# Attention quotients by compacting DMAs and a spreading product in place of transposes, with the jobs spread anew over the steps

## What is computed

```python
xn = layernorm(x)
q = rope(xn @ Wq); k, v = split(ctx @ Wkv); k = rope(k)
w = softmax(q k^T / 4)                    # per head, 256 x 256
attn = (w v) @ Wout + bout
x = x + tanh(g_xattn) * attn
h = layernorm(x)
y = square(relu(h @ up)) @ down + (h @ expert_weight) * (sum of the two largest of h @ gate)
out = x + tanh(g_ffn) * (layernorm(y) * gamma + beta)
```

## Time and profile before

| | |
|---|---|
| median of 3 runs | 1609.11 us (1608.59 to 1610.73) |
| profiled execution | 1609.51 us, its span 1607.7 us |
| mean granted clock of TensorE | 0.991 |
| PE busy | 1552.5 us, 97%, 9818 matmuls |
| DVE busy | 976.1 us, 61% |
| ACT busy | 638.1 us, 40% |
| POOL busy | 296.2 us, 18% |
| DMA | 119.50 MB in 67064 packets on SP's queue |
| first phase | to about 762 us, an iteration in its middle 44.96 us |

### The profile page before, as it was taken

One profiled execution on the slowest core, in us unless ns is written; L12 is line 12 of the kernel. 1 busy time (PEld: TensorE's weight loads), 2 busy tenths in 40 slices (PEclk: granted clock), 3 DMA queues, 4 the chain that ended last, 5 costly groups with the idle time before them and its releaser, 6 DMA issues.

```text
span 1607.7 us, 26049 instructions
## 1 busy us (share of the span) xinstructions
PE 1552.5 (97%) x9818; PEld 1158.5 (72%) x9818; DVE 976.1 (61%) x1448; ACT 638.1 (40%) x962; POOL 296.2 (18%) x370
## 2 busy tenths in 40 slices
PE   8799999999999999988999999999999999999997
PEld 6466666666666666654887887878878878788786
DVE  7887777887887777765663535426444354353524
ACT  4365555555555555556442222222222222222221
POOL 5222222222222222201010102002010020010202
PEclk9799999999999999999999999999999999999999
DMA  6644443444444344333530101101000011010101
GB/s 173 142 114 109 108 102 104 126 104 124 127 124 116 97 107 102 96 89 117 154 105 1 53 27 33 47 2 53 27 27 33 21 47 33 14 46 21 53 0 40
DMA packets 67192, 121.24 MB, mean 75 GB/s; under 512 B 12280, under 2 KB 25720, under 8 KB 67064
## 3 DMA queue, kind: packets, MB, share of 16 engines
q1 hardware_dynamic: 67064, 119.50, 27.8%
HBM read 51.17 MB, written 16.78 MB: 42 GB/s over the span
## 4 chain that ended last, share of the span: by engine, by line
PE 84%; DVE 11%; issue 2%; ACT 1%; POOL 1%; DMA 0%; POOLq 0%; DVEq 0%; ACTq 0%; SPq 0%
PE pP L986 16%; PE pA L1183 11%; PE pO L986 11%; PE pB L1183 11%; PE pT L986 10%; PE pO L1108 6%; PE pA L1080 6%; DVE mneg L1402 5%; PE pM L986 4%; PE pB L1096 2%; PE pT L993 2%; PE pP L993 2%; PE pM L993 2%; PE pM L1150 1%; DVE rot L1330 1%
## 5 line engine op out<-in xcount | busy, mean ns | idle before, releaser
L1402 DVE TENSOR_REDUCE mneg<-pA 128x4 f32<-128x1024 f32 x250 | 305.6, 1223 | 137.1 <-PE pA L1080 135.3
L887 ACT ACTIVATE probs<-pB 128x1024 f32<-128x1024 f32 x249 | 255.2, 1025 | 259.5 <-PE pB L1096 249.4
L1505 DVE TENSOR_TENSOR relu<-relu 128x512 f32<-128x512 f32 x128 | 89.0, 695 | 257.4 <-ACT hid L939 257.4
L704 POOL TENSOR_SCALAR var_eps<-meanvar 128x1 f32<-128x1 f32 x96 | 34.5, 360 | 1048.4 <-DVE meanvar L1287 1048.2
L1183 PE MATMUL pA<-dn,hid 128*128 128x512 f32 x768 | 198.6, 394 | 0.7
L1183 PE MATMUL pB<-dn,hid 128*128 128x512 f32 x768 | 196.0, 390 | 0.0
L986 PE MATMUL pP<-fT,up 128*128 128x512 f32 x768 | 190.3, 396 | 0.0
L986 PE MATMUL pO<-fT,up 128*128 128x512 f32 x768 | 187.6, 393 | 0.0
L1183 PEld LDWEIGHTS pA<-dn,hid 128*128 128x128 f32 x768 | 143.2, 188 | 35.7 <-DVE hid L1507 4.2
L986 PEld LDWEIGHTS pO<-fT,up 128*128 128x128 f32 x768 | 144.3, 188 | 32.6 <-issue 0.7
L1183 PEld LDWEIGHTS pB<-dn,hid 128*128 128x128 f32 x768 | 144.2, 188 | 31.0
(11 more groups left out here) (199 smaller groups left out, 1971.3 us busy)
## 6 DMA issues: line engine op xcount, KB each, us to landing
stk<-kT SPq DMA_DIRECT2D x180, 128.0 KB, 2.9
stq<-qT SPq DMA_DIRECT2D x180, 128.0 KB, 3.0
fres<-x_scratch SPq DMA_DIRECT2D x34, 256.0 KB, 2.8
xin<-x SPq DMA_DIRECT2D x32, 256.0 KB, 3.0
xres<-x SPq DMA_DIRECT2D x32, 256.0 KB, 3.3
x_scratch<-xres SPq DMA_DIRECT2D x32, 256.0 KB, 2.3
out<-y_s SPq DMA_DIRECT2D x32, 256.0 KB, 2.0
fx<-x_scratch SPq DMA_DIRECT2D x29, 256.0 KB, 2.7
```

What stands on the lines that cost most here:

```text
L704: nc.gpsimd.tensor_scalar_add(var_eps[:], meanvar[:, 1:2], EPS).then_inc(ve_made, 1)
L887: nc.scalar.activation(probs[:, s % 4, :, :, :].rearrange("p a b s -> p a (b s)"), psum[:, :, :], ACT.Exp).then_inc(exp_done, 1)
L1402: nc.vector.tensor_reduce(mneg[par][:, :, 2 * u:2 * u + 2].rearrange("p t q -> p q t"), psum[:, :, :].rearrange("p q (t k) -> p q t k", t= ...
L1505: nc.vector.tensor_tensor(r[:], r[:], r[:], ALU.mult).then_inc(sq_made, 1)
```

## The change

The numerators and denominators never leave the layout in which heads lie on partitions. For each half h of a batch (16 heads):

- `gather_den`, one DMA: the 16 denominator rows of `av_s` (4 partitions x 4 column blocks x 256) become `den`, 64 partitions x 64.
- `reciprocals` on DVE: three operations of 64x64 (reciprocal, rounded part, rest), in step 11 for half 0 and in step 3 of the next iteration for half 1.
- `scatter_recips`, two DMAs: rounded part and rest to 32 rows of 256 (`recips`).
- `move_av`, four DMAs: the 16 rows of numerators of each of the four heads in a column to every fourth partition of `numer`, so that 128 partitions are full.
- job b0 or b1 in bank T: two products of 256 columns of a 0/1 matrix (`spread`, 32 rows, made once by POOL) with `recips`. This copies each head's reciprocal onto its 16 partitions; hi and lo are added by the same product.
- DVE multiplies the bank by `numer` (in place), ACT rounds it (`round_av`, steps 4 and 8), POOL takes the rest (`rest_av`). O0 and O1 now take slices of the result, with the rows of Wout reordered on the host.

The jobs a00, a10, a01, a11, aT0, aT1 are gone, and O0, O1, V0, V1 have other steps. Some SBUF tiles have other places (`rot21`, the tiles of m's transposes, which now share their partitions with `recips` and `spread`, and the gate's weights); the two halves of a tile of raw weights lie in `numer`.

```diff
 SCHEDULE = {
-    0: ("X0", "a10"),
+    0: ("X0",),
     1: ("K0",),
-    2: ("Q0<", "a01"),
+    2: ("Q0<", "b0"),
     3: ("m1", "Q0"),
-    4: ("a11",),
+    4: ("V1",),
     5: ("X1", "kT0"),
-    6: ("aT0",),
+    6: ("b1",),
     7: ("K1", "Q1<"),
-    8: ("Q1", "O0<"),
-    9: ("kT1", "O0"),
+    8: ("Q1",),
+    9: ("kT1", "O0<"),
     10: ("qT0",),
-    11: ("aT1", "V1"),
+    11: ("O0",),
     12: ("m0", "qT1"),
-    13: ("O1",),
-    14: ("V0",),
-    15: ("a00",),
+    13: ("V0",),
+    14: ("O1<",),
+    15: ("O1",),
 }
+RECIPROCALS = {11: 0, 3: 1}
+ROUNDED = {4: 0, 8: 1}
...
+            def gather_den(b, h):
+                sp.wait_ge(av_taken, GROUPS * b + GROUPS // 2 * (h + 1))
+                if some(2 * b + h):
+                    sp.wait_ge(rc_in, 2 * INC * (2 * b + h))
+                    alone(sp)
+                sp.dma_start(den[:, :], av_s[HD:P:32, GROUPS // 2 * h:GROUPS // 2 * (h + 1), :]
+                             .rearrange("j g (r s) -> j (g r) s", r=4)).then_inc(den_in, INC)
+
+            def scatter_recips(b, h):
+                n = 2 * b + h
+                sp.wait_ge(rc_made, 3 * (n + 1))
+                if some(n):
+                    freed, of = ("b0", b) if h else ("b1", b - 1)
+                    sp.wait_ge(done[BANK[freed]], number(freed, of))
+                alone(sp)
+                for k, part in enumerate((den_hi, den_lo)):
+                    sp.dma_start(recips[NH // 2 * k:NH // 2 * (k + 1), :].bitcast(F32), part[:, :].bitcast(F32)).then_inc(rc_in, INC)
+
+            def move_av(b, h):
+                sp.wait_ge(av_taken, GROUPS * b + GROUPS // 2 * (h + 1))
+                if some(b):
+                    sp.wait_ge(done[BANK["O1"]], number("O1", b - 1))
+                alone(sp)
+                for j in range(MOVES):
+                    sp.dma_start(numer[j:P:4, 2 * h:2 * h + 2, :].rearrange("p c s -> p (c s)"),
+                                 av_s[32 * j:32 * j + HD, GROUPS // 2 * h:GROUPS // 2 * (h + 1), :]
+                                 .rearrange("d g s -> d (g s)")).then_inc(moved[h], INC)
...
+                if within(bt):
+                    gather_den(bt, 1)
                 if within(b1) and not opened("kT1", b1):
                     load_stack(b1, (par + 1) % 2, 1, "k")
+                if within(bt):
+                    scatter_recips(bt, 1)
+                    move_av(bt, 1)
+                if within(b1) and not opened("kT1", b1):
                     load_stack(b1, (par + 1) % 2, 1, "q")
...
+                gather_den(i, 0)
+                if within(b2):
+                    load_stack(b2, par % 2, 0, "k")
+                scatter_recips(i, 0)
                 if within(bt):
                     store_x1(bt, 0)
-                if within(b2):
-                    load_stack(b2, par % 2, 0, "k")
                 if within(b1):
                     load_max(b1, (par + 1) % 2, 0)
                 if within(b2):
                     load_stack(b2, par % 2, 0, "q")
+                move_av(i, 0)
                 if within(bt):
                     store_x1(bt, 1)
...
+            def rest_av(b, h):
+                pool.wait_ge(at_hi, 2 * b + h + 1)
+                cut = slice(2 * h, 2 * h + 2)
+                nc.gpsimd.tensor_tensor(aT_lo[:, cut, :], numer[:, cut, :], aT_hi[:, cut, :].bitcast(F32),
+                                        ALU.subtract).then_inc(at_lo, 1)
...
+                    for c in range(2):
+                        last = nc.tensor.matmul(psum[:, c * S:(c + 1) * S], spread[:, c, :], recips,
+                                                start=True, stop=True)
...
+                    nc.vector.tensor_tensor(numer[:, cut, :], psum.rearrange("p (c s) -> p c s", c=2), numer[:, cut, :],
+                                            ALU.mult).then_inc(freed, 1)
+
+            def reciprocals(b, h):
+                n = 2 * b + h
+                dve.wait_ge(den_in, INC * (n + 1))
+                alone(dve)
+                d = den[:, :]
+                nc.vector.reciprocal(d, d).then_inc(rc_made, 1)
+                dve.wait_ge(rc_made, 3 * n + 1)
+                nc.vector.tensor_copy(den_hi[:, :], d).then_inc(rc_made, 1)
+                dve.wait_ge(rc_made, 3 * n + 2)
+                nc.vector.tensor_tensor(den_lo[:, :], d, den_hi[:, :].bitcast(F32), ALU.subtract).then_inc(rc_made, 1)
```

More of the change, by code:

```diff
@@ L109 @@
 CUT = [x[:-1] for names in SCHEDULE.values() for x in names if x[-1] == "<"]
-TWO_STEP = ("X0", "X1", "qT0", "qT1", "kT0", "kT1", "aT0", "aT1", "m0", "m1")
+TWO_STEP = ("X0", "X1", "qT0", "qT1", "kT0", "kT1", "m0", "m1")
 ROPES = ("K0", "Q0", "K1", "Q1")
-A_JOBS = ("a00", "a10", "a01", "a11")
+R_AT = HALF_ROWS
+R_ROWS = 2 * NH // 2
+MOVES = 4
 X_AT = (6, 8, 10, 12)
@@ L261, in flamingo_gated @@
         raw1 = [probs[:, k // 2, k % 2, :, :].rearrange("p t s -> p (t s)") for k in range(8)]
-        raw1 += [attn[0][:], attn[1][:], xres[0][:], xres[1][:]]
+        raw1 += [numer[:, 2 * k:2 * k + 2, :].rearrange("p c s -> p (c s)") for k in range(2)]
+        raw1 += [xres[0][:], xres[1][:]]
         rot_k1 = raw1[0]
@@ L365, in flamingo_gated @@
         t_hi = sem("t_hi")
-        rd_made = sem("rd_made")
+        spread_made = sem("spread_made")
+        den_in = sem("den_in")
+        rc_made = sem("rc_made")
+        rc_in = sem("rc_in")
+        moved = [sem(f"moved{h}") for h in range(2)]
+        at_hi = sem("at_hi")
+        at_lo = sem("at_lo")
         res_in = [sem(f"res_in{t}") for t in range(2)]
@@ L736, in iteration @@
                 if prepares:
-                    for name in ROPES[1:]:
-                        rope_sum(b2, name)
+                    rope_sum(b2, "K1")
+                ending = isinstance(i, int) and i == B - 1
+                if ending:
+                    for u in range(2):
+                        inv_std(NT + u + 1)
+                if within(bt):
+                    rest_av(bt, 1)
+                if prepares:
+                    rope_sum(b2, "Q1")
                 if within(i + 3):
@@ L741, in iteration @@
                     split_ctx(i + 3, (par + 1) % 2)
-                if isinstance(i, int) and i == B - 1:
-                    for u in range(UT):
+                if ending:
+                    for u in range(2, UT):
                         inv_std(NT + u + 1)
@@ L1049, in compute @@
                 elif name[0] == "O":
-                    last = product(psum, lambda a, c: aT[a][:, c, :], lambda w, c: wo_s[w][:, c, :], KC, half)
+                    pe.wait_ge(at_lo, 2 * b + (1 if half == 0 else 2))
+                    cut = slice(t * P, (t + 1) * P)
+                    last = product(psum, lambda a, c: aT[a][:, c, cut], lambda w, c: wo_s[w][:, c, :], KC, half)
                 elif name[0] in "qk":
@@ L1202, in fblock @@
                     if first_block and m == 0:
-                        job("a10", B, B)
+                        job("b0", B, B)
                         pe.wait_ge(av_taken, GROUPS * B)
@@ L1206, in fblock @@
                     if first_block and m == 0:
-                        job("a01", B, B)
                         pe.wait_ge(gt_lo, 1)
@@ L1428, in iteration @@
                         ln_apply(i + 3, 0)
+                    if s in RECIPROCALS and within(i - RECIPROCALS[s]):
+                        reciprocals(i - RECIPROCALS[s], RECIPROCALS[s])
                     if planned(norm_at, i, s) is not None:
@@ L1464, in _ @@
             phase1(dve, iteration, ahead=1)
-            job("a00", B - 1)
+            job("O1", B - 1)
             split_gate()
-            job("a10", B)
+            job("b0", B)
             dve.wait_ge(av_done, GROUPS * B)
@@ L1500, in fblock @@
                     if first_block and m == 0:
-                        job("a01", B)
                         for key in ffn_chunks[4:ahead_w]:
```

109 lines of the change are left out of this document (67 added, 42 removed), and 8 rows, old and new, of tables (BANK, LAG).

## The result

The changed kernel takes 1724.91 us (median of 4 executions, 1723.67 to 1727.22) against 1609.55 us before (4 executions): ratio 1.072, 95% interval 1.0704 to 1.0736, so 7% slower. The profiled execution took 1723.87 us, 114.4 more than that of before, with a span of 1722.1.

A forecast was written before the change was run, and what follows sets the result against it. It took TensorE (PE), busy 97% of the span, as the bound. Terms -54 - 12 + 29 + 20 + 36 + 16 + 6 + 15 = +56 on 1609.51 gave 1665 us, range 1630 to 1682.

The forecast's parts named there:

- V0 behind qT1: Step 13, bank P: V0 waits 2.06 us for qT1's evacuation in 14 iterations, +29 us.
- V1 behind m1: Step 4, bank M: V1 waits 1.33 us for m1's evacuation, delayed by DVE's reciprocals, in 15 iterations, +20 us.
- SP's queue: Step 8's logits wait 2.8 us for m1's maxima copies, behind new DMAs, in 13 iterations, +36 us.
- The clock: Behind PE's new long waits the granted clock falls to 1.2 GHz: 9 falls of 1.7 us, +15 us.
- The count of one in three: Two of six earlier PE waits were followed by a clock fall, so 27 new waits over 2 us give 9.
- the clock falls at almost every long wait: Rival: 27 falls of 1.7 us cost 46 us in place of 15, giving 1696 us; chance 0.12.
- The PE work: Transposes that go save 61.3 us, 64 added products of 256 columns cost 7.3 us: -54 us.
- The two ends: Last two iterations, with step 8's copies late by about 5 and 11 us, +16; second phase's first block, +6 us.
- the old waits: Step 0's wait for maxima and step 5's for Q0's rotation go: 0.86 us in 14 iterations, -12 us.
- The rival that SP's chain is in time: m1's maxima copies land before step 8's logits need them, so that wait goes: 1612 us; chance 0.27.

The follow-up runs named there:

- the second run: The changed kernel with only V1's bank changed, from M to T: 1725.22 us, ratio 1.0709 to the kernel before.
- The version of 1599.56 us: Changed kernel with V0, V1 in bank T, m1's copies earlier on SP, residual adds behind Q1's sum, reciprocals in step 2, last iteration's loads and reciprocals reordered: ratio 0.9932.

## Why the prediction was wrong

The direction was right, the time was 60 us short, and the value lay outside the range. The waits were found and sized rightly; two terms of the sum were not: what the low clock costs, and what PE's work gives.

**V0 behind qT1**: 2.06 us x 14 forecast, 28.0 in 14 waits measured. **V1 behind m1**: 1.33 x 15 forecast, 17.7 in 14 measured, with DVE's three operations at 0.94 us where I took 0.85. **SP's queue**: 2.8 us x 13 forecast, 35.8 in 13 measured. From the first scatter (430.74) to the start of the last copy (442.4) SP took 11.7 us where I had 11.2, and that copy was used 2.0 us after its issue where I had 2.5: two errors that cancel, which is luck. The Trainium skill's 2.0 us (DMA: Bandwidth & Descriptors, "Anatomy of one DMA"), which I had weighed and not taken, agrees with these 2.0. Together 81.5 us in place of 85. But V1's 20 us are no cost of its place: the second run shows that without V1's wait step 8 waits that much longer. The sum of the waits stands all the same, since I had let V1's wait bring PE later to step 8.

**The clock, the first failed step**: "9 falls x 1.7 = +15 us". In the changed kernel's trace 9 of the 14 waits at V0 and all 14 at step 8 are followed by a stretch at 1.2 GHz (the last one is at 1.2 GHz from the start of its 3.84 us on, behind four waits of 0.8 to 1.1 us for the maxima). Between the start of V0's products and the start of the 16 of 256 columns behind them lie 3.63 us at 410.04 and 2.25 where the clock stayed up. The trace puts the price at 13.4 us behind V0 and some 28 behind step 8, 42 in place of 15: 23 stretches and not 9, at 1.5 us behind V0 and 2.0 on the mean behind step 8, where some last longer. So the count failed, and the 1.7 us for one fall was about right. The runs bear it out: 17 to 21 us and some 16 behind V0, some 28.5 behind step 8. The count of one in three came from six waits of 1.2 to 1.8 us, and I had applied it to waits of 2.0 to 3.8. V1's waits of 1.24 us are the counter-example in the same trace: the products behind them take 1.64 to 1.67 us every time. So the rival "the clock falls at almost every long wait" was the right one, with 23 of 28 and 42 us for its 46; my argument against it, that PE is full on both sides, did not hold.

**The PE work, the second failed step**: "-54 us". The change saves less of PE's time per iteration, not counting waits and the clock: 44.96 - 0.86 = 44.10 before; after, 51.24 less 5.8 of waits (2.00, 1.24, 2.38 and 0.18 for kT1) and 3.0 of low clock (4.72 - 3.25 and 5.63 - 4.1), 42.4. That is 1.7 us in place of 3.4 (54/16), 27 us over 16 batches. I had priced transposes by their busy time and the added products by the mean of a stream. From start to start, the four transposes of a job took 0.42 to 0.58 us in five of the six jobs that went, where the busy sum says 0.64; the two products of 256 columns took 0.43 (426.37 to 426.80 above), where I put 0.23; and cutting O1 in two added 0.2. With these three the saving would be some 2.2; what takes the rest isn't shown. The version of 1599.56 us, whose middle has no long wait, comes out near: an iteration of 42.80 us, of which 0.7 are small waits (for K1's sum and kT), leaves 42.1, so 2.0 saved. Its first rows on PE's timeline, of one iteration and of the next:

```profile
400.23 0.51 PE L1188 MATMUL pA<-stk,stq 48*128 48x256 f32 x4
...
443.03 0.51 PE L1188 MATMUL pA<-stk,stq 48*128 48x256 f32 x4
```

**The two ends**: 16 + 6 forecast; 14.6 in the last iteration, 3.8 in the wait of step 8 before it and 4.8 behind, 23. The sum was near, by luck, since the place was not: I had step 8's copies late by 11 us, while the long wait is for the first tile of the second phase, which stands ahead of them in the same queue. Part of the 23 is again low clock: behind 820 us PE works 20.3 us at 1.2 GHz, where the kernel before works 3.4 us at 1.2 GHz in its last iteration; if its work takes twice as long there, that is an estimated 8 us. (These first loads are 11 DMAs and took 7.5 us before, from 725.64 on, where my sum has 8.4.)

**The sum by these sizes**: 81.5 + 42 - 27 - 11 + 23 = 108.5, of 114.4. The 11 are the old waits, 12 in the forecast: PE's waits for the maxima and for Q0's rotation were 16.1 us between 100 us and the last iteration, and 5.3 are left. Of the other 6 us, 2.5 are kT1's small waits; the rest I can't place.

**The rival that SP's chain is in time** fell: the wait was there in every iteration. The end that it named, 1612, was wrong as the forecast's was: the runs that remove that wait, by SP's order or by reciprocals a step earlier, end at 1667 and 1668. What it said that the wait is worth, 53 us, was near: these runs gained 57.5 and 56.5.

## What to carry to other kernels

Price PE work from start to start on the timeline, in the step where it stands, and not by the busy sum of a group. In this kernel, whose PE is full, a new wait of 2 us and more cost itself and most of the time 1.5 to 2 us of low clock behind it. So count such a wait at nearly double until a trace says otherwise, and put useful work there or move the job to another bank. When a DMA queue gets new entries, order it by who waits and how soon, and follow each entry that moves back to its reader and to what stands behind that reader; then look at the last iteration by itself.

## What the runs showed of the hardware

I had not expected that added work could shorten a kernel: 14 transposes whose result nobody reads, in place of most of each 2.0 us of idle time, gave 14.9 us. Nor that equal waits can differ: of 14 waits of 2.00 us before the same six products, nine were followed by the low clock and five were not, and over the six traces in which this wait stands 62 of 84 were; what sets these apart stays open. And a wait need not be that long: with the reciprocals a step earlier, step 8 still waits 1.4 to 1.7 us in three places, and all three are followed by 1.2 GHz, while V1's 1.24 us never are. A reciprocal of 64x64 took 0.54 us in one instruction, where one of 128x16, with half as many elements and a quarter as many in a partition, took 0.245.
